# A decoder layer in one kernel: the routing of the chosen tokens moved into the feed-forward's last block

## What is computed

```python
shared_out = einsum(ln(silu(h@sw1.T+sb1) * (h@sw2.T+sb2)), sw3) + sb3        # all 4096 rows, H=256
x_moe = h[index_b, index_t]                                                  # the 1024 chosen rows
shared_scores = sigmoid(x_moe @ sg_w.T + sg_b)
expert_scores = sigmoid(x_moe @ eg_w.T + eg_b)                               # 8 experts
top1_idx   = argmax(expert_scores + exp_bias); top1_score = expert_scores[top1_idx]
weights    = softmax([shared_scores, top1_score])
expert_out = the same feed-forward with the weights of expert top1_idx       # H=256
final_out  = shared_out.at[index_b, index_t].set(shared_out[...]*weights[0] + expert_out*weights[1])
```

## Time and profile before

| | |
|---|---|
| median of 3 runs (lowest, highest) | 3127.72 us (3125.29, 3130.46) |
| the profiled execution: its own time, span of its trace | 3130.21 us, 3128.1 us |
| PE busy, share of the span | 2911.1 us, 93% |
| DVE, ACT, POOL busy | 67%, 51%, 56% |
| mean DMA rate | 137 GB/s |
| self-attention, by its 2048 reductions on DVE (L825) | 1269.6 us busy |

### The profile page before, as it was taken

How to read it: one execution, slowest core, us unless ns; L and a number is a source line. 1 busy time by engine, 2 the same in 40 slices (tenths; PEclk the granted TensorE clock), 3 DMA queues, 4 the chain that set the end, 5 groups by cost and what they waited for, 6 DMA issues and landing times. The chain is left out here.

```text
span 3128.1 us, 41596 instructions
## 1 busy us (share of the span) xinstructions
PE 2911.1 (93%) x15224; PEld 1729.2 (55%) x15224; DVE 2080.9 (67%) x3801; ACT 1608.6 (51%) x2998; POOL 1739.8 (56%) x747
## 2 busy tenths in 40 slices
PE   8999799999999999999999999979969997999477
PEld 5888455555555555555555555448845554777333
DVE  4332577777777777777777777545629895776323
ACT  2222066666666666666666666732227673222111
POOL 1000178889898989898989898820021101442366
PEclk9999599999999999999999999999979998999679
DMA  6544835465566564655665646356566552343531
GB/s 221 187 172 153 216 78 119 95 142 126 123 131 132 116 142 106 143 124 123 132 132 115 139 109 149 75 156 193 174 151 161 135 152 96 135 162 122 201 92 38
DMA packets 179393, 427.50 MB, mean 137 GB/s; under 512 B 30046, under 2 KB 51455, under 8 KB 156093
## 3 DMA queue, kind: packets, MB, share of 16 engines
q1 hardware_dynamic: 154614, 279.05, 30.8%
q0 software_dynamic: 24288, 145.27, 22.5%
q10 hardware_dynamic: 288, 0.52, 0.1%
HBM read 180.67 MB, written 118.79 MB: 96 GB/s over the span
## 5 line engine op out<-in xcount | busy, mean ns | idle before, releaser
L825 DVE TENSOR_REDUCE part_max<-ps_s 128x1 f32<-128x512 f32 x2048 | 1269.6, 682 | 371.7 <-PE ps_s L713 371.6
L925 ACT ACTIVATE probs<-ps_st 128x512 f32<-128x512 f32 x2048 | 1058.0, 602 | 491.2 <-PE ps_st L732 477.2
L660 POOL TENSOR_TENSOR added<-added,probs 128x2048 f32<-128x2048 f32 x251 | 1168.9, 4657 | 71.9 <-ACT probs L925 48.7
L732 PE MATMUL ps_st<-q_stack,k_stack 98*128 98x512 f32 x2048 | 865.0, 425 | 10.5 <-ACT probs L925 9.0
L713 PE MATMUL ps_s<-k_stack,q_stack 96*128 96x512 f32 x2048 | 826.6, 410 | 17.0 <-DMA k_stack<-k_lo 17.0
L732 PEld LDWEIGHTS ps_st<-q_stack,k_stack 98*128 98x128 f32 x2048 | 386.9, 190 | 519.3 <-ACT probs L925 369.4
L743 PE MATMUL ps_pv<-probs,v_sb 128*32 128x512 f32 x4096 | 546.3, 605 | 0.0
L713 PEld LDWEIGHTS ps_s<-k_stack,q_stack 96*128 96x128 f32 x2048 | 396.3, 194 | 111.0 <-DVE part_max L825 30.1
L668 POOL DMA_DIRECT2D probs<-probs x128 | 111.3, 869 | 182.9 <-PE ps_pv L743 178.3
L743 PEld LDWEIGHTS ps_pv<-probs,v_sb 128*32 128x32 f32 x4096 | 80.7, 108 | 163.2 <-ACT probs L925 137.3
L660 POOL TENSOR_TENSOR added<-probs 128x2048 f32<-128x2048 f32 x32 | 146.6, 4581 | 10.1 <-ACT probs L925 9.9
(11 more groups left out here) (282 smaller groups left out, 3555.5 us busy)
## 6 DMA issues: line engine op xcount, KB each, us to landing
probs<-probs POOLq DMA_DIRECT2D x128, 1024.0 KB, 7.1
q_stack<-q_hi SPq DMA_DIRECT2D x64, 256.0 KB, 5.2
k_stack<-k_hi SPq DMA_DIRECT2D x64, 256.0 KB, 6.2
xq_stack<-q_parts SPq DMA_DIRECT2D x32, 512.0 KB, 4.9
q_parts<-k_stack SPq DMA_DIRECT2D x60, 256.0 KB, 4.0
x_in<-in_x_rows SPq DMA_DIRECT2D x8, 1024.0 KB, 8.2
q_hi<-qk_h_out SPq DMA_DIRECT2D x8, 1024.0 KB
q_lo<-qk_l_out SPq DMA_DIRECT2D x8, 1024.0 KB
```

Of the source, the lines that this page charges most:

```text
L660: pool.tensor_tensor(added[:, w % 2], left, probs[:, k % RING], ALU.add).then_inc(added_up, 1)
L732: pe.matmul(ps_st[:, n % BANKS], k_stack[0:TOP, w // BPB, j, k * P:(k + 1) * P], q_stack[:, w % 4, j], start=True, stop=True).then_inc(ite ...
L825: dve.tensor_reduce(part_max[:, s:s + 1], ps_s[:, (w * SLOTS + s) % BANKS], AX.X, ALU.max)\
L925: act.activation(probs[:, k % RING, j], ps_st[:, n % BANKS], ACT.Exp, scale=SCALE).then_inc(item_used, 1)
```

## The change

Steps 1 to 5 of the serial part move into the feed-forward stage.

- Its small loads and the fill of the slot table are issued by SP after the first block's h rows.
- In the last block POOL gathers the chosen rows ahead of `z_affine`, into the space of `a_raw`, and scatters the payload after it. PE does the gate after the last up-projection and ahead of the first z transposes, with one PSUM buffer for the transposed tile (two before) and one addition of the bias for all tiles. DVE and ACT have the choice, the counting and the slots interleaved with the block's splits, copies and outputs, in an order written out by hand (`last_body`).
- The experts' stage starts with loads of the weights of experts 0 and 1 from ACT's queue; SP loads the slot table when the scatters have landed (semaphore `table_scattered`, kept over the barrier) and then the weights of experts 2 to 7, w12 and w3 of an expert together. PE waits at step s only for the weights of expert s.
- Every expert is given at least one tile (the last line of the diff), so that tile s never belongs to an expert later than s.

```diff
+        h_sel = a_raw[:].rearrange("p u c k -> p (u c) k")
+        ht = x_in[:, 0, 0:2].rearrange("p b (c t) -> p b c t", t=P)
...
                 advance(0, 0, True)
+                sp.dma_start(idx_b[:], index_b).then_inc(idx_loaded, 16)
+                sp.dma_start(idx_t[:], index_t).then_inc(idx_loaded, 16)
+                for dst, source in ((gate_sb[:], gate_t.rearrange("(c p) n -> p c n", p=P)),
+                                    (gate_bias_all[:], gate_bias.partition_broadcast(P)),
+                                    (exp_bias_all[:], exp_bias.partition_broadcast(P)), (ramps[:], ramp), (before_sb[:], before)):
+                    sp.dma_start(dst, source).then_inc(route_loaded, 16)
+                sp.wait_ge(route_consts, 1)
+                sp.dma_start(slot_table.rearrange("(p j) c -> p j c", p=P), blank[:].bitcast(F32)).then_inc(blanked, 16)
...
+                def gather_chosen():
+                    for s in range(2):
+                        pool.wait_ge(h_stored[s], 16 * NBLK // 2)
+                    pool.wait_ge(idx_done, 5)
+                    for m in range(MT):
+                        pool.indirect_dma_start(h_sel[:, m], None, h_rows,
+                                                bass.IndirectOffsetOnAxis(row_idx[:, m:m + 1], axis=0)).then_inc(h_gathered[m], 16)
+
+                def scatter_slots():
+                    pool.wait_ge(blanked, 16)
+                    pool.wait_ge(placed, 4)
+                    for m in range(MT):
+                        pool.indirect_dma_start(slot_table, bass.IndirectOffsetOnAxis(slot_i[:, m:m + 1], axis=0),
+                                                payload[:, m], None).then_inc(table_scattered, 16)
+
                 def body(i, u, last):
+                    if last:
+                        gather_chosen()
                     z_affine(i, u)
+                    if last:
+                        scatter_slots()
...
+                pool.wait_ge(bo_added, 2 * TPB)
+                pool.memset(blank[:], NO_ROW).then_inc(route_consts, 1)
+                pool.wait_ge(route_consts, 1)
+                pool.memset(ones_sb[:], 1.0).then_inc(route_consts, 1)
+                pool.wait_ge(route_consts, 2)
...
+                def rows_of_tokens():
+                    dve.wait_ge(idx_loaded, 2 * 16)
+                    dve.tensor_scalar(wrap_b[:], idx_b[:], 0, B, ALU.is_lt, ALU.mult).then_inc(idx_done, 1)
+                    dve.tensor_scalar(wrap_t[:], idx_t[:], 0, S, ALU.is_lt, ALU.mult).then_inc(idx_done, 1)
+                    dve.wait_ge(idx_done, 2)
...
+                    for buf in sums + tile_sums:
+                        dve.memset(buf[:], 0.0).then_inc(route_cleared, 1)
+                    dve.wait_ge(idx_done, 5)
+                    dve.tensor_copy(payload[:, :, 0].bitcast(I32), row_idx[:]).then_inc(placed, 1)
+                    dve.memset(payload[:, :, 3], 0.0).then_inc(placed, 1)
...
+                def logits_out():
+                    dve.wait_ge(route_loaded, 5 * 16)
+                    dve.wait_ge(logits_in_psum, MT)
+                    dve.tensor_tensor(logits[:], ps_p[:, 1, 0:MT * G].rearrange("p (m g) -> p m g", g=G),
+                                      gate_bias_all[:].unsqueeze(1).to_broadcast([P, MT, G]), ALU.add).then_inc(biased_logits, 1)
...
+                def choose_experts():
+                    dve.wait_ge(scored, 1)
+                    dve.tensor_tensor(biased[:], scores[:, :, 1:G], over_tiles(exp_bias_all[:]), ALU.add).then_inc(routed, 1)
...
+                def give_slots():
+
+                    dve.wait_ge(route_cleared, 8)
+                    dve.wait_ge(counted, 1)
+                    totals = ps_p[:, 0, MT * E:2 * MT * E].rearrange("p (m e) -> p m e", e=E)
+                    dve.tensor_copy(sums[0][:, 4:], totals).then_inc(mapped, 1)
...
+                def last_body(i, u):
+                    rows_of_tokens()
+                    gate(i, u, True)
+                    logits_out()
+                    z_split(i, u, 0)
+                    z_split(i, u, 1)
+                    choose_experts()
+                    output(i, u, 0)
+                    z_split(i, u, 2)
+                    give_slots()
+                    output(i, u, 1)
+                    z_split(i, u, 3)
+                    output(i, u, 2)
+                    output(i, u, 3)
+
                 def body(i, u, last):
+                    if last:
+                        return last_body(i, u)
...
+                def last_body(i, u):
+                    for m in range(MT):
+                        act.wait_ge(ht_in_psum, m + 1)
+                        if m >= 2:
+                            act.wait_ge(logits_in_psum, m - 1)
+                        act.activation(ht[:, m % 2], ps_p[:, 0].rearrange("p (c t) -> p c t", t=P), ACT.Copy).then_inc(ht_copied, 1)
+                    z_high(i, u, 0)
+                    z_high(i, u, 1)
+                    act.wait_ge(biased_logits, 1)
+                    act.activation(scores[:], logits[:], ACT.Sigmoid).then_inc(scored, 1)
+                    shared(i, u, 0)
+                    act.wait_ge(routed, 9)
+                    act.activation(top_score[:], top_score[:], ACT.Exp).then_inc(exped, 1)
+                    z_high(i, u, 2)
+                    shared(i, u, 1)
+                    z_high(i, u, 3)
+                    shared(i, u, 2)
+                    shared(i, u, 3)
...
+                def logits_of(m):
+                    pe.wait_ge(ht_copied, m + 1)
+                    for c in range(DC):
+                        mm = pe.matmul(ps_p[:, 1, m * G:(m + 1) * G], ht[:, m % 2, c], gate_sb[:, c], start=(c == 0), stop=(c == DC - 1))
+                    mm.then_inc(logits_in_psum, 1)
+
+                def last_body(i, u):
+
+                    pe.wait_ge(resid_done, NBLK * TPB)
+                    pe.wait_ge(route_loaded, 5 * 16)
+                    for m in range(MT):
+                        pe.wait_ge(h_gathered[m], 16)
+                        if m:
+                            pe.wait_ge(ht_copied, m)
+                        for c in range(DC):
+                            mm = pe.transpose(ps_p[:, 0, c * P:(c + 1) * P], h_sel[:, m, c * P:(c + 1) * P], ident[:])
+                        mm.then_inc(ht_in_psum, 1)
+                        if m:
+                            logits_of(m - 1)
+                    logits_of(MT - 1)
+                    z_transposes(i, u, 0)
+                    z_transposes(i, u, 1)
+                    down(i, u, 0)
+                    pe.wait_ge(route_consts, 2)
+                    pe.wait_ge(routed, 6)
+                    choices = one_hot[:].rearrange("p m e -> p (m e)")
+                    pe.matmul(ps_p[:, 0, 0:MT * E], before_sb[:], choices, start=True, stop=True)
+                    pe.matmul(ps_p[:, 0, MT * E:2 * MT * E], ones_sb[:], choices, start=True, stop=True).then_inc(counted, 1)
+                    z_transposes(i, u, 2)
+                    down(i, u, 1)
+                    z_transposes(i, u, 3)
+                    down(i, u, 2)
+                    down(i, u, 3)
...
-        w12_loaded, w3_loaded = sem("w12_loaded"), sem("w3_loaded")
...
+        small_loaded, ident_loaded, ramps_loaded = sem("small_loaded"), sem("ident_loaded"), sem("ramps_loaded")
+        w_loaded = [sem(f"w_loaded{e}") for e in range(E)]
...
+        SMALL = 3
+        BY_ACT = 2
+
+        def load_weights(engine, e):
+            engine.dma_start(w12[:, e], w12_t[e].rearrange("(c p) n -> p c n", p=P)).then_inc(w_loaded[e], 16)
+            engine.dma_start(w3[:, e], w3_t[e].rearrange("(c p) n -> p c n", p=P)).then_inc(w_loaded[e], 16)
...
-                sp.wait_ge(h_gathered[MT - 1], 16)
-                for e in range(E):
-                    sp.dma_start(w12[:, e], w12_t[e].rearrange("(c p) n -> p c n", p=P)).then_inc(w12_loaded, 16)
-                for e in range(E):
-                    sp.dma_start(w3[:, e], w3_t[e].rearrange("(c p) n -> p c n", p=P)).then_inc(w3_loaded, 16)
-                sp.wait_ge(scattered_slots, 16 * MT)
+                sp.wait_ge(table_scattered, 16 * MT)
                 sp.dma_start(slots[:], slot_table.rearrange("(j p) c -> p j c", p=P)).then_inc(slots_loaded, 16)
+                for e in range(BY_ACT, E):
+                    load_weights(sp, e)
...
-                pool.memset(blank[:], NO_ROW).then_inc(consts, 1)
                 pool.memset(minus_half[:], -0.5).then_inc(consts, 1)
-                pool.memset(ones_sb[:], 1.0).then_inc(consts, 1)
+                pool.wait_ge(consts, 1)
                 pool.memset(bias_rows[:].bitcast(F32), 0.0).then_inc(consts, 1)
-                pool.wait_ge(idx_done, 5)
-                for m in range(MT):
-                    pool.indirect_dma_start(h_sel[:, m], None, h_rows,
-                                            bass.IndirectOffsetOnAxis(row_idx[:, m:m + 1], axis=0)).then_inc(h_gathered[m], 16)
-                pool.wait_ge(consts, 4)
```

(30 more changed lines are left out.)

307 lines of the change are left out of this document (134 added, 173 removed).

## The result

The changed kernel took **3110.9 us** (median of 5 runs, 3109.1 to 3113.8) against 3127.7: ratio 0.9936, 95% interval 0.9925 to 0.9947. It is 16.9 faster where 27.4 was forecast, and inside the range of 3091 to 3114. The quotient of the two medians alone is 0.9946, at the edge of that interval; by the ratio itself the gain is 20. Its profiled execution has a span of 3108.7.

The account below looks back on a forecast made before the run. A chain of waits was taken as the bound, with a serial stretch before the experts' tile loop. 34.4 - 2 - 2.5 - 2.5 = 27.4 off the profiled 3130.2 gives 3102.8, less 2.5 to the median: 3100.3 us; range 3091 to 3114.

Parts of the forecast that it names:

- The table's load 34.4 earlier: Start of the experts' stage: the slot table's load is issued at 2943.1 instead of 2977.46, 34.4 us earlier.
- The gather and the index arithmetic at no cost: Last feed-forward block: index arithmetic and eight gathers hide behind the up-projections, so PE waits for no gather; 0 us.
- DVE ready ahead of the tiles: Experts' stage: DVE's clears, choice of experts and split biases end at 2953.6, with 3.5 us of cover.
- the term for the table's load: Experts' stage: weights moving beside the table's load make it land 2 us later, bounds 0 to 5.
- The loop's term: Tile loop: gathers of tiles 2 to 4 land later beside the weights, 2.5 us in all, bounds 0 to 10.
- The sum: Whole kernel: 34.4 less 2, 2.5 and 2.5 for contention gives a gain of 27.4 us.
- Rival A: Gate: PE's clock holds, so it takes 11.6 us instead of 18.0; total 3094; chance 0.17.
- B: Experts' stage: gathers queue behind the weights, contention 24.7 instead of 7, gain 9.7 us; total 3118; chance 0.13.
- C: Tile loop: PE loses its clock, 3.6 us a step; gain of 27 gone after eight steps, ten give 3136; chance 0.03.
- D: The last block grows by as much as the next stage loses, so nothing is gained; total 3128; chance 0.04.
- No weight is late: Tile loop: each expert's weights take 4.5 us and are due 9.4 us apart on average, so none is late.
- The sign of being wrong that I had named: Tile loop: a wait of PE on h_in over 4 us past tile 4, or on a weight.

Follow-up runs that it names:

- stores_alone: Changed kernel, but POOL's scatters into the table wait until the last block's stores have landed; 3127.4 us, ratio 0.9980.
- act_waits: Changed kernel, but ACT holds the weights of experts 0 and 1 until the slot table has landed; 3109.1 us, ratio 0.9930.
- both: Changed kernel with the table's load ahead of SP's five small loads and ACT's weights held until it has landed; 3107.5 us, ratio 0.9921.
- weights_all: Changed kernel, but PE waits for all experts' weights ahead of the loop, as before the change; 3129.3 us, ratio 0.9988.
- warm: dve_split with dummy matmuls in PE's waits for gathered tiles, their results overwritten; 3106.2 us, ratio 0.9916.
- ring4: dve_split with four h_in buffers for gathered tiles instead of three; 3095.1 us, ratio 0.9886.
- ring4_alone: Changed kernel with four h_in buffers for gathered tiles as its only edit; 3103.6 us, ratio 0.9908.
- table_first: Changed kernel with the slot table's load ahead of the five small loads in SP's queue; 3104.3 us, ratio 0.9912.
- dve_split: Changed kernel with table first on SP, all weights behind it there, and DVE clearing only 3 tiles of acc before the choice of experts; 3101.6 us, ratio 0.9900.

## Where the prediction was right and wrong

- **The table's load 34.4 earlier: right (34.6), by errors that cancel.** The gate took 15.0 and not 18.0: PE kept the full clock up to the fifth tile's logits and then lost it. PE's timeline, the last up-projection, then the logits of the first tile, the sixth, and the last two:

```profile
2894.17 1.08 PE L2243 MATMUL e_ps_f<-xwo_w_h,e_xt_l 128*128 128x512 f32 x4
...
2896.93 0.96 PE L2275 MATMUL e_ps_p<-gate,e_x_in 128*128 128x9 f32 x8
...
2904.38 1.71 PE L2275 MATMUL e_ps_p<-gate,e_x_in 128*128 128x9 f32 x8
...
2906.83 3.42 PE L2275 MATMUL e_ps_p<-gate,e_x_in 128*128 128x9 f32 x16
```

  Payload (26.5 against 29.4), the last scatter (36.3 against 40.1) and the last store (31.4 against 34.6) follow. But from the last store to the next stage it took 2938.42-2926.62 = 11.8 and not the 7.8 of the earlier trace rows: the stores landed late beside the scatters, 2.9 of the 4.0 by stores_alone. The gate's 3 us and the stores' 4 the other way cancel by luck: so the stage starts at 43.2, forecast 43.1.
- **The gather and the index arithmetic at no cost: right** (tile 0's transposes directly behind the last up-projection; PE waited 0.78 for ACT's copy only).
- **DVE ready ahead of the tiles: right, with a wrong part.** I let the 1.55 us gap before the `acc` memset vanish. It is there with POOL idle, and it grows with the memset: gap and duration together are 1.61 us for 1536 elements a partition, 6.52 for 6144 and 8.01 for 7680, about 1.05 ns an element each time. DVE was ready at 58.4 (56.5 forecast), and the second tile landed at 65.5, 7 us later.

```profile
2942.78 6.46 DVE L2489 MEMSET acc<- 128x7680 f32 x1 [1.55 <-issue]
```
- **The step that failed is the term for the table's load: 2, measured 8.8.** I took its bounds as 0 and 5, the end of ACT's 9 us of weights; it went beyond even the upper one. The 9 us were too few: ACT's weights moved until 2951.5, 13.1 after their first issue, with SP's loads beside them (my own numbers gave their end as 2949.3 and not 2951). The table's rows were done at 2952.0. They take 3.1 to 3.2 us alone, and here they waited behind SP's slowed broadcasts and then moved at a third of their speed. The scatter's 5.90 under load, 128 rows, was no measure of 1920. From the Trainium skill's rule in the prediction (each engine alternates between queues packet by packet) I had drawn that the terms are small. The rows moved do look like turns taken, 585 of ACT's beside the table's 1920; what fails is my step from turns to a small term, because 1920 rows need many turns. With 128 rows the second tile's gather took 5.87, and I had 5.93.
- **The loop's term: 2.5, measured 5.7.** I had named the gathers of tiles 2 to 4. Of these only tile 3's was late by the change, 1.5 us more of waiting. The other 2.6 of waiting lie later in the loop, and the 3.0 of lower clock at its two ends, none of which I had.
- **The sum: 27.4 forecast, 17.6 in the profile.** The table's load lacks 6.8 and the loop 3.2, and the earlier load gives back 0.2. That it lay inside the range is owed to the range, which was made wide for contention.
- **Rival A**: came true for five tiles of eight, and the gate took 15.0, between its 11.6 and my 18.0. **B**: its gain of 9.7 is nearer to the measured 16.9 than my 27.4, but not by its cause: the gathers landed in 5.9, not behind the weights, and it had the table's load at 5 more. **C**: the clock did cost more, 3.0 us and not its 27, and not after gaps for a gather. **D**: out by the result, whose interval ends at 0.9947.
- **No weight is late: right** in the changed kernel (no wait of PE on `f_w`), not when ACT's weights are held back (4.5 us in the loop of act_waits, 1.6 in that of both). The sign of being wrong that I had named, a wait for `h_in` over 4 us past tile 4, did not come: the longest there is 2.4.

**Open.** Why the waits for `h_in` past tile 3 are 2.6 us longer than before, also without weights beside them (12.7 in all in weights_all). What decides whether a memset holds a gather's issue. And the gate: 15.0 in eight profiles of the changed routing, but 20.5, 19.2, 22.3 and 19.0 in those of warm, ring4, stores_alone and ring4_alone, whose code up to there is the same. In these four ACT's first copy started late, PE waited 1.5 to 3.2 instead of 0.78, and the lower clock came 3.6 to 5 us behind U instead of 8. As in ring4_alone:

```profile
2898.18 0.63 PE L2287 MATMUL e_ps_p<-e_identity,e_a_raw 128*128 128x128 f32 x4 [1.54 <-issue]
...
2901.06 1.09 PE L2287 MATMUL e_ps_p<-e_identity,e_a_raw 128*128 128x128 f32 x4
```

What delays that copy is not shown. The four also ran on two chips of their own, so the chip can't be told from the version here. In these four profiles the gate cost 4 to 7 us; whether the other executions of these versions paid it too is not known.

## What to carry to other kernels

When a wait is removed, ask what was already waiting behind it: here a slow table load, a memset that held POOL's gather issue and expert 0's weights lay close behind each other, and the best single edit among them got 6 us. A load of many tiny rows belongs on an empty DMA path, here 3 us instead of 8 to 12, so put it ahead of the weights and hold the bulk behind it. And look at a loop's own waits before counting it as unchanged: one buffer more for the gathered tiles took nearly 12 us off the loop, about as much as the last block's interleaving, and 7 us off the median.

## What the runs showed of the hardware

- Loading 30 KB as 1920 rows of 16 bytes: 3.1 to 3.2 us alone, 4.6 behind five small loads, 8.4 and 11.5 to 11.9 beside 3.1 MB of weights from ACT's queue. The rows themselves moved in 1.4 us alone, and in 4.4 to 7.0 beside those weights.
- The first gather's issue on POOL took 7.84 instead of about 1.05 us beside a 6.46 us float32 memset on DVE, and ended 1.06 after it, as in act_waits and both. Other gathers beside such memsets (table_first, dve_split, the kernel before) took 0.94 to 1.05.
- A float32 memset on DVE takes about 1.05 ns an element of a partition, if the gap that the timeline shows ahead of it is counted in (8.01 us for 7680).
- The last store of 1 MB landed in 9.5 us beside scatters of 16-byte rows, in 6.6 without them.
- PE lost its clock in the gate without a pause: the windows view of the changed kernel has PE busy throughout, at 0.99 and then at 0.50. In the kernel before it stayed at 0.50 while busy for 12.70 of 13 us.

```profile
2897.00:2903.50 6.50, 6.50 (x57) 6.27 (x57) 2.76 (x9) 2.99 (x5) 5.13 (x7) 0.99 0.17 49
2903.50:2910.00 6.50, 6.50 (x33) 6.50 (x33) 0.00 (x0) 1.20 (x2) 1.74 (x3) 0.50 0.01 3
```
